# A projection's high part written once to both of its places in a DRAM image, with the image rows reordered

## The reference

```python
x = L0_attn_x                                  # (8, 512, 256)
xn = _layernorm(x)
s = attention0(xn)      # 16 query heads of 16, 4 key heads, distance bias, causal
g = _silu(ffn0(xn))     # 1024 hidden, Hadamard transform before the down projection
x = x + s * g
xn = _layernorm(x)
s = attention1(xn)      # 32 half heads of 8 in pairs, difference of two softmaxes, causal
g = _silu(ffn1(xn))     # shared expert of 352 and 8 experts of 176, top 2
x = x + s * g
```

## Time and profile before

| | |
|---|---|
| median of 3 runs | 2339.62 us |
| profiled execution: time / span | 2333.17 / 2331.4 us |
| PE busy | 2123.6 us (91% of the span) |
| DVE, ACT, POOL busy | 1381.2, 893.0, 665.6 us |
| chain that ended last | PE 69%, DMA 7%, DVE 7%, SPq 4% |
| granted TensorE clock, mean | 0.965 of full speed |
| setup, up to the first score matmul | 121.66 us |
| a batch | about 278 us |

### The profile page before, as it was taken

How to read it: one execution, slowest core, us unless ns; L and a number is a source line. 1 busy time by engine, 2 the same in 40 slices (tenths; PEclk the granted TensorE clock), 3 DMA queues, 4 the chain that set the end, 5 groups by cost and what they waited for, 6 DMA issues and landing times.

```text
span 2331.4 us, 33812 instructions
## 1 busy us (share of the span) xinstructions
PE 2123.6 (91%) x12386; PEld 1435.3 (62%) x12386; DVE 1381.2 (59%) x2705; ACT 893.0 (38%) x1749; POOL 665.6 (29%) x831
## 2 busy tenths in 40 slices
PE   2389999989999999998999999999999999999998
PEld 1247557575666656675575755657556665666656
DVE  3565565656656666655657566565665666665664
ACT  2142452515524353333524245251452425433352
POOL 2332331313313232223313233141331323222331
PEclk7599999999999999999999999999999999999999
DMA  6813423243131532216231352324313253231530
GB/s 204 294 48 99 156 67 105 73 140 104 52 107 62 177 93 78 81 46 181 92 94 52 95 161 68 105 64 141 106 55 102 71 158 101 63 88 55 179 95 14
DMA packets 105604, 240.51 MB, mean 103 GB/s; under 512 B 17048, under 2 KB 27288, under 8 KB 105184
## 3 DMA queue, kind: packets, MB, share of 16 engines
q1 hardware_dynamic: 91184, 194.41, 27.6%
q0 software_dynamic: 14256, 43.94, 6.2%
HBM read 179.67 MB, written 57.82 MB: 102 GB/s over the span
## 4 chain that ended last, share of the span: by engine, by line
PE 69%; DMA 7%; DVE 7%; SPq 4%; ACT 3%; issue 3%; POOL 1%; DVEq 0%; ACTq 0%; POOLq 0%
PE bank L393 19%; PE bank L552 12%; PE bank L473 11%; PE bank L442 9%; PE bank L489 9%; PE bank L446 3%; DMA qring<-mneg 3%; DMA upring<-up_img 3%; PE bank L571 2%; SPq L351 2%; DVE nmax L724 2%; PE bank L499 1%; DMA k_img<-probs 1%; DVE probs L740 1%; ACT probs L630 1%
## 5 line engine op out<-in xcount | busy, mean ns | idle before, releaser
L724 DVE TENSOR_REDUCE nmax<-bank 128x1 f32<-128x512 f32 (+3 forms) x1056 | 651.7, 640 | 328.1 <-PE bank L446 315.2
L393 PE MATMUL bank<-xnT,upring 128*128 128x512 f32 (+1 forms) x2208 | 632.1, 409 | 24.5 <-DMA upring<-up_img 23.8
L630 ACT ACTIVATE probs<-bank 128x512 f32<-128x512 f32 (+1 forms) x864 | 469.0, 559 | 348.7 <-PE bank L473 335.1
L473 PE MATMUL bank<-qring,kring 128*128 128x512 f32 (+1 forms) x1056 | 476.9, 455 | 55.4 <-ACT probs L630 24.5
L442 PE MATMUL bank<-kring,qring 127*128 127x512 f32 (+3 forms) x1536 | 459.7, 352 | 32.9 <-DMA kring<-k_img 25.9
L393 PEld LDWEIGHTS bank<-xnT,upring 128*128 128x128 f32 x2208 | 402.2, 195 | 106.4 <-issue 32.0
L442 PEld LDWEIGHTS bank<-kring,qring 127*128 127x128 f32 x1536 | 271.3, 194 | 111.3 <-DVE nmax L724 52.6
L552 PE MATMUL bank<-wdown,hbuf 128*128 128x256 f32 x1408 | 327.5, 382 | 0.0
L473 PEld LDWEIGHTS bank<-qring,kring 128*128 128x128 f32 x1056 | 206.6, 197 | 190.3 <-ACT probs L630 100.3
L1505 POOL TENSOR_SCALAR_AFFINE_SELECT probs<-probs 128x512 f32<-128x512 f32 x256 | 162.5, 635 | 517.4 <-ACT probs L630 514.9
L552 PEld LDWEIGHTS bank<-wdown,hbuf 128*128 128x128 f32 x1408 | 260.2, 191 | 32.7 <-issue 1.7
(11 more groups left out here) (119 smaller groups left out, 1525.7 us busy)
## 6 DMA issues: line engine op xcount, KB each, us to landing
upring<-up_img SPq DMA_DIRECT2D x176, 512.0 KB, 4.4
q_img<-probs SPq DMA_DIRECT2D x96, 256.0 KB, 3.1
qring<-q_img SPq DMA_DIRECT2D x256, 64.0 KB, 1.9
kring<-k_img SPq DMA_DIRECT2D x64, 256.0 KB, 3.1
qring<-q_img SPq DMA_DIRECT2D x32, 384.0 KB, 4.6
k_img<-probs SPq DMA_DIRECT2D x48, 256.0 KB, 4.6
up_img<-hbuf POOLq DMA_DIRECT2D x22, 512.0 KB, 5.1
gring<-gate_img POOLq DMA_DIRECT2D x32, 256.0 KB, 3.7
```

What stands on the lines that cost most here:

```text
L393: last = nc.tensor.matmul(out_ap, part_a(a, pa, k), part_b(b, pb, k), start=(n == 0), stop=(n == len(steps) - 1))
L473: nc.tensor.matmul(SC[n % 2][:, 0:heads * w].rearrange("p (g n) -> p g n", g=heads), kring[l][:, ks, kt * P:(kt + 1) * P], qring[l][:, s, ...
L630: nc.scalar.activation(pr, pr if biased else scores, ACT.Exp, scale=scale).then_inc(s_exp, 1)
L724: nc.vector.tensor_reduce(nmax[:, u % 2, g0:g0 + heads, qt], MX[n % 2][:, 0:heads * w].rearrange("p (g n) -> p g n", g=heads), AX.X, ALU.m ...
```

## The change

`write_images` issues two transfers for a tile in place of three. The first writes the high part to both of its places: its source has a dimension of size 2 with step 0, so each row of SBUF is read twice. The second writes the low part. To make one pattern reach both places, the rows of an image are no longer ordered by part and then dimension (`d * t + i`) but by dimension and then part (`i * 3 + t` in layer 0, `i * 4 + t` in layer 1). q and k are reordered alike, so the products that are summed stay the same. The leading dimension of the written pattern is now one row of the tile (`(h d)`, 128 or 64) and no longer the head (8, 4 or 16). Each image's semaphore counts 32 and no longer 48. The padding rows of layer 1 become every fourth row. The last row of a head (31) is a padding row in both orders, so the row of ones and the row of maxima stay where they are.

```diff
-        s_img = [[sem(f"image_written_{l}_{i}", 48) for i in range(tiles[l])] for l in (0, 1)]
+        s_img = [[sem(f"image_written_{l}_{i}", 32) for i in range(tiles[l])] for l in (0, 1)]
...
                 img = (q_img if is_q else k_img)[l][h0:h0 + m // d]
                 sp.wait_ge(s_phi[l], so_far(s_phi[l], i + 1))
-                for t, part in ((0, 0), (1, 0), (2, 1)) if is_q else ((0, 0), (2, 0), (1, 1)):
-                    if part:
-                        sp.wait_ge(s_plo[l], so_far(s_plo[l], i + 1))
-                    sp.dma_start(img[:, d * t:d * t + d, :], stage(i, part)[0:m, :]).then_inc(s_img[l][i], 16)
+                high, low = (slice(0, 2), 2) if is_q else (slice(0, 3, 2), 1)
+                rows = img.rearrange("h (d t) n -> (h d) t n", d=d)
+                sp.dma_start(rows[:, high, :], stage(i, 0)[0:m, :].unsqueeze(1).to_broadcast([m, 2, T]))\
+                    .then_inc(s_img[l][i], 16)
+                sp.wait_ge(s_plo[l], so_far(s_plo[l], i + 1))
+                sp.dma_start(rows[:, low, :], stage(i, 1)[0:m, :]).then_inc(s_img[l][i], 16)
...
-                        nc.gpsimd.dma_start((q_img, k_img)[t - 4][1][:, 24:32, :], zero_t).then_inc(s_pad, 16)
+                        nc.gpsimd.dma_start((q_img, k_img)[t - 4][1][:, 3:32:4, :], zero_t).then_inc(s_pad, 16)
```

More of the change, by code:

```diff
@@ L309, in wait_images @@
             for i in range(tiles):
-                eng.wait_ge(s_img[l][i], so_far(s_img[l][i], 48))
+                eng.wait_ge(s_img[l][i], so_far(s_img[l][i], 32))
         def wait_images_before(eng):
             for s in s_img[0]:
-                eng.wait_ge(s, before(s, 48))
+                eng.wait_ge(s, before(s, 32))
         def mx(u):
```

## The result

The changed kernel takes 2284.57 us (median of 4 runs, 2283.36 to 2287.99), the kernel before 2341.46 us (its median here, over 4 runs).

A forecast was written before the change was run, and what follows sets the result against it. The prediction took PE, busy 91% of the span, as the bound, image writes mattering only where PE waits behind them. Setup -13, batch ends -1 and layer 1 front -4 made -18 us: 2339.6 to about 2321 us, range 2298 to 2335.

The forecast's parts named there:

- Setup, -13 us: Setup: image writes spread over 16 engines, so unit 0's ring lands and the setup ends 13 us earlier (7.8 to 16).
- Rival 2: Setup: its loop was bound by DMA, so only about 5 us remain there; 2330 us, chance 0.14.
- End of a batch, -1 us: Ends of seven batches: images land some 5 us earlier, but PE computes meanwhile; only ring waits of 1.1 us go.
- Front of layer 1, -4 us: Layer 1 front, eight batches: 3 us for small gaps in the feed and 1 us for the clock.
- they then only wait longer in the queue: Layer 1 front: SP reaches tile 13's weights 1.5 to 2.5 us earlier, but they gain only queueing time.
- the weights stand behind the same bytes in either kernel: Layer 1 front: tile 13's weights queue behind unchanged traffic, in a window with a DMA share of 0.97.
- SP issues 256 KB in 0.6 us, 430 GB/s, faster than DMA moves it: Layer 1 front: SP's issue is not the limit, so the landing of tiles 0 and 1 hardly moves.
- -1 us for the clock: Layer 1 front: 1 us gained in the 12 matmuls behind the wait for tile 13's weights.
- the main forecast: Whole kernel: gains in setup, batch ends and layer 1 front give 2321 us, own range 2313 to 2330, chance 0.60.
- Rival 1: Layer 1 front: SP's issue holds tile 13's weights back, so 28 us go in place of 4; 2297 us, chance 0.14.
- Rival 3: Layer 1 image writes: rows 8 KB apart run a quarter slower; 2360 us, chance 0.06.
- Rival 4: Image writes: the doubled read gains no engines or is served as two transfers; nothing moves, 2339 us, chance 0.06.

The follow-up runs named there:

- layer 0 alone: The kernel before with the new writes in layer 0 only, layer 1 keeping the old ones: 2327.04 us, ratio 0.9949.
- layer 1 alone: The kernel before with the new writes in layer 1 only, layer 0 keeping the old ones: 2300.17 us, ratio 0.9833.
- the streams: Program without the computation: SP writes four tiles back to back, twice, in each form of image write; layer 1's old form ran at 263 GB/s.
- extra issues: The changed kernel with four more one-row transfers (8 KB in all) behind tile 3's image in layer 1: 2293.45 us, ratio 0.9818.
- the run with extra bytes: The changed kernel with two more 256 KB transfers to a spare place behind tile 3's image in layer 1: 2302.53 us, ratio 0.9854.

## Why the prediction was wrong

**Setup, -13 us: right in its mechanism, 2.5 us too much.** The wait of 24.8 us became 12.0, as forecast, and the leading dimension is the cause: layer 0 alone gives it (11.5), layer 1 alone leaves it at 23.7, and three transfers with leading 128 and 64 give it too (13.3). The writes by themselves show half the engines for a leading 8 (share 0.47) and a quarter for 4 (0.23). The step "I take the whole 13 us as moved to the end of the setup" was wrong: 10.5 arrived. The engines are full up to 57 us now and POOL waits 5.45 us for a stored tile, which fits, but isn't shown to be the reason. Rival 2 argued so and had too small a number.

**End of a batch, -1 us: right.** The ring waits of 1.1 us went, and PE's own work covered the rest.

**Front of layer 1, -4 us: this step failed.** It measured -34.4 us (range given: 0 to -28). The size of the lead was forecast well: SP should reach tile 13's weights 1.5 to 2.5 us earlier, and as a mean it does so by 2.29. What failed is the sentence behind it, "they then only wait longer in the queue". It held for 0.82 us of 2.97 in batch 0: the weights are issued 2.97 us earlier relative to the first image and land 2.15 earlier, and the window of that landing has a share of 0.66, not a full queue.

The step rested on two readings. One was "the weights stand behind the same bytes in either kernel", with a share of 0.97 and a full rate of 289 GB/s. The bytes are the same, but a share counts engines that are busy, and how much they move isn't in it. The old writes run at 263 GB/s in the streams, the new ones at 300 to 312, with the share within 0.03. The other was "SP issues 256 KB in 0.6 us, 430 GB/s, faster than DMA moves it", so that SP's issue couldn't be the limit. Tile 3's image took 0.99 us for each 256 KB in the same rows, and SP issues in 11.42 of the 11.79 us between the ring and tile 13's weights.

The Trainium skill ("DMA: Bandwidth & Descriptors", the section on why a DMA increments its semaphore by 16) would give leading 16 and leading 128 the same 16 engines. The equal shares of the streams agree with it. How many engines it feeds was the only thing that I asked of the leading dimension, and in layer 1 that answer was "no change".

A row of this case spoke against the step and was read only as half an argument: one window had a share of 0.93 at 174 GB/s. I used it for a rival in which writes get slower, and not for one in which they get faster.

The last part, -1 us for the clock, was 14.25: in seven of eight batches the 12 matmuls behind the wait took 4.40 to 5.46 us, and with the waits at most 1.46 us all eight take 3.0. The step gave this term 1 us although its own rows had one slow batch (5.46) and one fast one (3.00), and it weighed no others. (The lower end given for the main forecast, 2313, comes out at 2314.6 from its own terms; nothing hangs on that.)

**Rival 1 (SP's issue holds the weights, 2297 us)** came nearest in time, and its sign that the waits fall below 12 us came true. As a mechanism it is right in part. SP's time alone, put back by extra issues, brings 7 us of waits back and costs about 9; SP's time and the rate together, put back for q by a leading 16, cost 20 to 27. It priced the waits and the clock at 28 us, and they are 34.4. It had a chance of 0.14, and the range left its lower half out. **Rival 3 (slower by scattered writes)** is refuted: rows 8 KB apart are written at 303 GB/s, faster than the old form. A contiguous piece reaches 329, so the scattering does cost about 8%, and the leading dimension gives back 12%. **Rival 4** is refuted by the shares at the batch's end.

What stays open: why a leading 16 streams slower than 128 at an equal share, and why it costs SP more to issue. The experiments vary it and show its price, in isolation and in place, but none looks inside a transfer, and none splits layer 1's gain between the rate and SP's issuing, since the leading dimension changes both. Also open is the share of the third transfer itself, between 0 and 15 us.

## What to carry to other kernels

Read a DMA share together with the GB/s beside it. A full share at 289 GB/s is not the ceiling while another window of the same kernel shows 414, and the first thing to vary is the leading dimension of the pattern. Take rates over whole stretches, not from one microsecond. Look also at whether the issuing engine pauses at all between two transfers that matter. Where PE waits 1.5 to 4 us at the same place in each batch, read all the batches, price the wait and the half clock behind it together, and test the landing alone by moving that one transfer in the list; here that move gave some 32 us, where layer 1's new writes give 39.

## What the runs showed of the hardware beyond that

- Leading 16 against 128, 128 rows of 2 KB: 263 and 303 GB/s, shares 0.82 and 0.84, issue 0.61 and 0.43 us each.
- Leading 8 and 4: 167 and 85 GB/s, shares 0.47 and 0.23.
- A tile of 64 rows moves at 169 GB/s with a share of 0.78, where the same form with 128 rows has 326 at 0.87. In the changed kernel 213 GB/s at 0.97 stand at the end of a batch, behind the issues of the k tile of layer 0, but a window in layer 1 has 217 at 1.08, so there it isn't shown to be the tile's doing.
- PE idle for 3.54 us is followed by a granted clock of 0.50 for 5.46 us; idle for 1.46 us, by 1.00. The length of the wait alone doesn't decide it: in the run with extra bytes the matmuls behind a wait of 3.26 us took 2.97 us at 1.00, and before, a wait of 2.04 us was followed by 4.57 us at 0.63 on average.
- Issuing: four transfers of one row (2 KB) each took SP 2.60 us in the front part, three of 256 KB with leading 128, first in that part, 1.29.
